# A relational graph network on one core: each node's edge to itself computed on chip, and ScalarE's copies of finished rows put ahead of the next tile's second exp

## The reference, cut to what matters

```python
for l in range(L):
    ht = jnp.einsum('nd,rdo->nro', h, W_rel[l])
    msg = ht[src, etype]
    h_rel = segment_sum(msg, dst) + h @ W_loop[l] + b_rel[l]
    z  = (h @ W_gat[l]).reshape(n, H, DH)
    el = sum(z * attn_l[l], -1);  er = sum(z * attn_r[l], -1)
    e  = leaky_relu(el[src] + er[dst], 0.2)
    ex = exp(e - segment_max(e, dst)[dst])
    h_gat = segment_sum(ex / denom * z[src], dst) + b_gat[l]
    hc = concat([h_rel, h_gat]) @ W_fuse + b_fuse
    if l == 0: hc = hc * sigmoid(concat([hc, mean(edge_weight)]) @ W_gate + b_gate)
    h = relu(hc)
x = layernorm(x + h)
```

## Time and profile before

| | us |
|---|---|
| time, median of 3 runs | 3487.19 (3486.21 to 3488.84) |
| profiled execution, span from first to last instruction | 3490.2 |
| POOL busy | 2489.3 (71%) |
| DVE busy | 2380.3 (68%) |
| PE busy | 689.4 (20%) |
| ACT busy | 424.8 (12%) |

### The profile page before, as it was taken

One profiled execution on the slowest core, in us unless ns is written; L12 is line 12 of the kernel. 1 busy time (PEld: TensorE's weight loads), 2 busy tenths in 40 slices (PEclk: granted clock), 3 DMA queues, 4 the chain that ended last, 5 costly groups with the idle time before them and its releaser, 6 DMA issues.

```text
span 3490.2 us, 18122 instructions
## 1 busy us (share of the span) xinstructions
PE 689.4 (20%) x1897; PEld 372.5 (11%) x1897; DVE 2380.3 (68%) x3226; ACT 424.8 (12%) x769; POOL 2489.3 (71%) x2642
## 2 busy tenths in 40 slices
PE   8942111222122230011121111221000000000000
PEld 5421000111011110000000000110000000000000
DVE  8536666677676764665777756674776788877786
ACT  3530110111111120101111111111000000000000
POOL 1457777777777756777777777775777777777776
PEclk9965555555655555555555555555555555555555
DMA  7774444455545544444454544454433333333332
GB/s 271 315 249 129 134 147 152 152 151 152 152 152 159 168 145 118 130 151 152 151 152 151 153 152 152 152 173 140 107 106 107 107 106 107 106 106 107 106 103 74
DMA packets 143244, 505.96 MB, mean 145 GB/s; under 512 B 44277, under 2 KB 51002, under 8 KB 133618
## 3 DMA queue, kind: packets, MB, share of 16 engines
q0 software_dynamic: 130032, 444.45, 43.4%
q1 hardware_dynamic: 13186, 61.24, 4.5%
HBM read 341.05 MB, written 164.51 MB: 145 GB/s over the span
## 4 chain that ended last, share of the span: by engine, by line
POOL 45%; issue 29%; DVE 10%; DMA 6%; PE 4%; POOLq 3%; DVEq 1%; ACT 1%; SPq 1%; ACTq 0%
POOL meta_nat L594 20%; POOL late L594 14%; POOL scratch L594 10%; DVE acc L1381 3%; PE ps_table L886 1%; DMA late<-table,stage_mid 1%; DMA table<-rows 1%; DMA scratch<-table,stage_tail 1%; DVE late L1377 1%; DVE scratch L1377 1%; DVE meta_nat L1377 1%; POOLq L369 1%; POOL table L671 1%; DMA meta_nat<-table,stage_head 1%; PE ps_cnt L919 1%
## 5 line engine op out<-in xcount | busy, mean ns | idle before, releaser
L594 POOL DMA_INDIRECT meta_nat<-table,stage_head x1200 | 1139.0, 949 | 395.7 <-issue 385.3
L594 POOL DMA_INDIRECT late<-table,stage_mid x720 | 681.9, 947 | 219.4 <-issue 217.9
L594 POOL DMA_INDIRECT scratch<-table,stage_tail x555 | 525.9, 948 | 175.5 <-issue 175.2
L1025 PE MATMUL ps_mix<-ident,hr 128*128 128x128 f32 x75 | 35.5, 473 | 1991.2 <-DVE hg L1401 1991.2
L788 ACT ACTIVATE ps_cnt<-logit 128x68 f32<-128x68 f32 x189 | 43.7, 231 | 2767.1 <-DVE logit L1363 2766.1
L1381 DVE TENSOR_REDUCE acc<-meta_nat 128x132 f32<-128x2112 f32 x75 | 290.6, 3875 | 8.1 <-DVE meta_nat L1377 0.5
L1371 DVE TENSOR_REDUCE acc<-meta_nat 128x128 f32<-128x2048 f32 x75 | 282.6, 3767 | 0.0
L1049 PE MATMUL ps_table<-wrel,hT 128*128 128x512 f32 x400 | 266.4, 828 | 0.0
L1353 DVE TENSOR_TENSOR raw<-late,er_cur 128x64 f32<-128x64 f32 x45 | 12.0, 267 | 324.5 <-DMA late<-table,stage_mid 324.5
L1025 PEld LDWEIGHTS ps_mix<-ident,hr 128*128 128x128 f32 x75 | 13.6, 182 | 2039.8 <-DVE hg L1401 2039.8
L1381 DVE TENSOR_REDUCE acc<-scratch 128x132 f32<-128x1188 f32 (+1 forms) x69 | 208.7, 3024 | 7.1
(11 more groups left out here) (237 smaller groups left out, 1701.4 us busy)
## 6 DMA issues: line engine op xcount, KB each, us to landing
table<-rows SPq DMA_DIRECT2D x25, 2080.0 KB, 7.7
meta_nat<-table,stage_head POOLq DMA_INDIRECT x1200, 2.8
late<-table,stage_mid POOLq DMA_INDIRECT x720
scratch<-table,stage_tail POOLq DMA_INDIRECT x555, 2.8
meta<-meta_ranked SPq DMA_DIRECT2D x1, 2438.0 KB, 15.1
wrel<-in_L_gnn_W_rel POOLq DMA_DIRECT2D x2, 1024.0 KB, 13.5
meta_nat<-in_x SPq DMA_DIRECT2D x1, 832.0 KB, 18.4
table<-rows,stage_id POOLq DMA_INDIRECT x50, 7.8
```

Source lines behind the costliest of these rows:

```text
L594: pool.indirect_dma_start(out=slots[b][:, k, :], out_offset=None, in_=table[l % 2], in_offset=bass.IndirectOffsetOnAxis(ap=index, axis=0)) ...
L1025: pe.transpose(mix[0], hr[:], ident[:])
```

## The change

Self edges are no longer gathered, except those of tile 0.

- While lists are prepared, DVE finds each node's last code, tests whether it is the node's own and whether its rank is at least 128, lowers the degree by one, puts the null row in its place and keeps the type in a new column `M_SELF`.
- The loop over all ranked tiles ahead of the layers is gone. In its place stands `first_layer_own`, which makes for one tile er, its own row of z and all 16 table products again from x, in ranked order. It runs for tiles 0 and 1 ahead of layer 0, and inside layer 0 at the end of each tile t for tile t+1.
- Of the 16 table products in PSUM, ACT keeps the one of the node's self type: 16 copies with a per-partition scale of 0 or 1 (`own_messages`). PE adds them and `h @ W_loop` in PSUM, 17 products (`own`), and ACT copies the sum to `meta` (`own_sum`). In layers 0 and 1 the same is done for the next layer, behind `next_rows`.
- The node's own z row is copied into slot 0 of H, which was unused, and the H group now has 17 slots in its logits and weighted sums.
- `next_rows` moves in ACT's order ahead of the exp of the second group. `s_rows` is incremented before the own copies.
- `z_product` of `next_table` is 136 columns wide rather than 264. The output buffer `yo` lies on `wrel`.

```diff
 (ACT)
-            act.wait_ge(s_meta, 16)
-            transposed_x(1)
-            for t in range(T):
-                if t < T - 1:
-                    transposed_x(t % 2)
-                act.wait_ge(s_er_ps, t + 1)
-                s.activation(meta[:, t, M_ER:META], ps_er[t % 2], ACT.Copy).then_inc(s_er, 1)
+            def own_er_and_z(t):
+                s.activation(meta[:, bass.ds(t, 1), M_ER:M_LOOP], ps_z[:, EL:ER]..., ACT.Copy)
+                s.activation(self_z[:, bass.ds(t, 1), :], ps_z[:, 0:EL]..., ACT.Copy)
+                s.activation(type_cur[:]..., self_type[:, bass.ds(t, 1), :], ACT.Copy)
+                s.activation(shut_cur[:], no_self[:, bass.ds(t, 1)], ACT.Copy).then_inc(s_type_cur, 1)
+                act.wait_ge(s_type_cur, n_own)
+                return s.activation(self_z[:, bass.ds(t, 1), DH:EL:EX], ps_z[:, DH:EL:EX]..., ACT.Identity,
+                                    bias=shut_cur[:])
+            def own_messages():
+                for r in range(R):
+                    m = s.activation(self_rows[:, r], ps_table[:, r * D:(r + 1) * D], ACT.Copy,
+                                     scale=type_cur[:, r:r + 1])
+                m.then_inc(s_masked, 1)
+            def own_sum(t, ready):
+                act.wait_ge(s_own_ps, n_own)
+                act.reg_add(n_own, n_own, 1)
+                s.activation(meta[:, bass.ds(t, 1), M_LOOP:META], self_sum..., ACT.Copy).then_inc(ready, 1)
+            def first_layer_own(t):
+                s.activation(x_cur[:]..., meta[:, bass.ds(t, 1), M_X:M_ELL], ACT.Copy).then_inc(s_x_cur, 1)
+                act.wait_ge(s_rank_xT, n_first)
+                s.activation(hT[1][:], xT_ranked, ACT.Copy).then_inc(s_hT[1], 1)
+                act.wait_ge(s_first_ps, n_first)
+                act.reg_add(n_first, n_first, 1)
+                own_er_and_z(t).then_inc(s_er, 1)
+                own_messages()
+                own_sum(t, s_own0)
...
                     s.activation(rows[0][:, :, D:ROW], bc(ps_z[:, 0:D + H], R), ACT.Copy)
-                    for j in range(2):
-                        evacuate_half(0, j)
-                    s.activation(meta[:, bass.ds(t, 1), M_ER:META], ps_z[:, D + H:ZW]..., ACT.Copy).then_inc(s_rows, 1)
+                    evacuate_half(0, 0)
+                    evacuate_half(0, 1).then_inc(s_rows, 1)
                     act.reg_add(n_tab, n_tab, 1)
+                    own_er_and_z(t)
+                    own_messages()
...
                     gate(l)
+                    next_rows(l, act.snap(n_last, min_val=0, max_val=T - 1))
                 with act.If(groups > 1):
                     group()
                     with act.If(groups > 2):
                         group()
-                if not first:
-                    next_rows(l, act.snap(n_last, min_val=0, max_val=T - 1))
-                    act.reg_add(n_last, n_last, 1)
...
+                elif l < L - 1:
+                    own_sum(act.snap(n_last, min_val=0, max_val=T - 1), s_own)
+                    act.reg_add(n_last, n_last, 1)
...
+            first_layer_own(0)
+            first_layer_own(1)
+            act.wait_ge(s_meta, 16)
...
+                if l == 0:
+                    with act.Fori(1, T - 1) as t:
+                        tile(l, t)
+                        first_layer_own(t + 1)
+                    tile(l, T - 1)
 (PE)
+            def own(l, k):
+                pe.wait_ge(s_masked, n_own)
+                pe.reg_add(n_own, n_own, 1)
+                pe.matmul(self_sum, hT[k][:], wz[:, l, ER:ZW], start=True, stop=False)
+                for r in range(R):
+                    mm = pe.matmul(self_sum, ident[:], self_rows[:, r], start=False, stop=r == R - 1)
+                mm.then_inc(s_own_ps, 1)
+            def first_layer_own():
+                pe.wait_ge(s_x_cur, n_x_cur)
+                pe.reg_add(n_x_cur, n_x_cur, 1)
+                pe.transpose(xT_ranked, x_cur[:], ident[:]).then_inc(s_rank_xT, 1)
+                pe.wait_ge(s_hT[1], n_hT[1])
+                pe.reg_add(n_hT[1], n_hT[1], 1)
+                pe.matmul(ps_z[:, 0:ER], hT[1][:], wz[:, 0, 0:ER], start=True, stop=True)
+                for c in range(4):
+                    mm = pe.matmul(ps_table[:, 512 * c:512 * c + 512], hT[1][:],
+                                   wrel[:, 0, c * RC * D:(c + 1) * RC * D], start=True, stop=True)
+                mm.then_inc(s_first_ps, 1)
+                own(0, 1)
...
                     pe.reg_add(n_tab, n_tab, 1)
+                    own(l + 1, 0)
...
-            for l in range(L):
+            with pe.Fori(2, T):
+                tile(0)
+                first_layer_own()
+            tile(0)
+            tile(0)
+            for l in range(1, L):
 (DVE, list preparation; lists and own are views of one chunk of tiles)
-                v.tensor_scalar(meta_nat[:, t0:t1, M_ELL:SCATTERED], ..., float(NULL), None, ALU.add).then_inc(s_ell_ok, 1)
+                step(v.tensor_tensor(codes, lists, is_last[:, t0:t1], ALU.mult))
+                step(v.tensor_reduce(code, codes, AX.X, ALU.add))
+                step(v.tensor_tensor(gap, code, self_at[:, t0:t1], ALU.subtract))
+                step(v.tensor_tensor(dropped[:, t0:t1], gap, gap, ALU.mult))
+                step(v.scalar_tensor_tensor(own, dropped[:, t0:t1], 0.25 * R * R, may_drop[:, t0:t1], ALU.is_lt, ALU.mult))
+                step(v.tensor_tensor(dropped[:, t0:t1], code, own, ALU.mult))
+                v.tensor_tensor(codes, is_last[:, t0:t1], bc_last(dropped[:, t0:t1], ELL), ALU.mult)
+                v.scalar_tensor_tensor(gap, gap, 0.5 * (R + 1), own, ALU.add, ALU.mult)
+                step(v.tensor_tensor(degree[:, t0:t1], degree[:, t0:t1], own, ALU.subtract))
+                v.tensor_scalar(meta_nat[:, t0:t1, M_SELF], gap, -1.0, None, ALU.add)
+                v.tensor_copy(meta_nat[:, t0:t1, M_CNT], degree[:, t0:t1])
+                v.scalar_tensor_tensor(lists, lists, float(NULL), codes, ALU.add, ALU.subtract).then_inc(s_ell_ok, 1)
 (DVE, layers; group works on slots 0 to K for H where it took 1 to K)
+                v.tensor_copy(slots["H"][:, 0:1, D:ROW], self_z[:, bass.ds(t, 1), :])
...
+                if l == 0:
+                    dve.wait_ge(s_own0, n_t)
```

More of the change, by code:

```diff
@@ L21 @@
 LEAST = -1.0e37
+SHUT = -1.0e34
 SLOPE = 0.2
@@ L46, in gnn_kernel @@
     META = M_LOOP + D
-    ZW = D + H + H + D
+    EL = D + H
+    ER = EL + H
+    ZW = ER + D
     HB = 25
@@ L121, in gnn_kernel @@
         rows = [sb(f"rows{i}", [P, R, ROW]) for i in range(2)]
+        self_z = rows[1][:].rearrange("p r f -> p (r f)")[:, 0:T * EL].rearrange("p (t f) -> p t f", f=EL)
+        assert T * EL <= R * ROW
+        self_rows = sb("self_rows", [P, R, D])
+        self_room = self_rows[:].rearrange("p r d -> p (r d)")
+        is_last = self_room[:, 0:T * ELL // 2].bitcast(BF16).rearrange("p (t j) -> p t j", t=T)
+        last_at, self_at, apart, may_drop, last_code, is_self, dropped = (
+            self_room[:, T * ELL // 2 + i * T:T * ELL // 2 + (i + 1) * T] for i in range(7))
+        assert T * ELL // 2 + 7 * T <= R * D
+        self_type = sb("self_type", [P, T, R])
+        no_self = sb("no_self", [P, T])
+        type_cur = sb("type_cur", [P, R])
+        shut_cur = sb("shut_cur", [P, 1])
+        x_cur = attn_tmp
         degree = sb("degree", [P, T])
@@ new lines, in own_messages @@
+            def own_messages():
[6 more added lines that the diff above has]
+                act.reg_add(n_own, n_own, 1)
+                s.activation(meta[:, bass.ds(t, 1), M_LOOP:META], self_sum.rearrange("p (o f) -> p o f", o=1), ACT.Copy
+                             ).then_inc(ready, 1)
@@ L859, in _ @@
                 tile(l, 0, first=True)
-                with act.Fori(1, T) as t:
-                    tile(l, t)
+                if l == 0:
[3 more added lines that the diff above has]
+                    tile(l, T - 1)
+                else:
+                    with act.Fori(1, T) as t:
+                        tile(l, t)
                 transposed(l)
@@ L864, in _ @@
                 gate(l)
-                next_rows(l, T - 1)
+                if l < L - 1:
+                    next_rows(l, T - 1)
+                    own_sum(T - 1, s_own)
         @block.tensor
@@ L998, in _ @@
                 natural_tile(t, t % 2, next_x=t < T - 1)
[L1001 to L1017 removed]
+            def first_layer_own():
[10 more added lines that the diff above has]
+                own(0, 1)
+            n_x_cur = counter(pe, "pe_x_cur", 1)
+            pe.wait_ge(s_rows, T + 1)
+            first_layer_own()
+            first_layer_own()
             pe.wait_ge(s_bload, 16 * (5 + 3 * L))
@@ L1173, in _ @@
             v.tensor_copy(meta_nat[:, :, M_START], starts[:])
-            step(v.tensor_tensor(ell_valid, bc(iota_slot[:], T), bc_last(degree[:], ELL), ALU.is_lt))
+            v.tensor_tensor(ell_valid, bc(iota_slot[:], T), bc_last(degree[:], ELL), ALU.is_lt)
```

(14 more changed lines are left out.)

87 lines of the change are left out of this document (52 added, 35 removed).

## The result

| | before | after |
|---|---|---|
| time, median us | 3486.7 (3485.4 to 3488.8, 4 runs) | 3531.7 (3526.9 to 3538.0, 4 runs) |
| ratio, 95% interval | | 1.0133 (1.0118 to 1.0147), slower |
| profiled execution, span | 3490.2 | 3525.3 |
| POOL, DVE, PE, ACT busy | 2489, 2380, 689, 425 | 2421, 2386, 1204, 804 |

The change costs 45.0 us by the runs and 35.1 by the two spans; the profiled execution after is the fastest of its four. The forecast was 3541, slower.

What follows compares the result with a forecast made beforehand. POOL's time to start DMAs was taken to bound the kernel before, with a longer ACT and PE chain in most layer 0 tiles after. -90 + 124 + 9 + 7 + 4 = +54 us, so 3541 us, range 3450 to 3630.

Steps and rivals of the forecast that it cites:

- Gathers, -90: All three layers: 24 fewer gathers in each, 72 x 1.252 = 90.1 us of POOL saved; layer 2 shows 28 to 31.
- Layer 0, +124 -30 = +94: Layer 0: an ACT and PE chain of 46 us (47.5 with three groups) exceeds POOL's time in 18 tiles, +124 us.
- the faster rival: Layer 0: PE at full clock everywhere and copies 0.17 us apart give a chain of 36 us; chance 0.24.
- The masked copies: ACT's 16 masked copies in layer 0: 0.25 us apart, the last 0.35, 4.1 us a set; bounds 2.7 and 5.8.
- Start, +9: Before layer 0: two own tiles put the first exp at 253 us, +9 us, bounds 2 and 14; list steps hidden.
- Ends, +7 and +4: Ends of layers 0 and 1: +7 us as the second exp waits for `next_rows`, and +4 us; bounds -5 and 15.
- The move of `next_rows`: ACT's order in the loops: the reorder alone costs nothing; a few us in each last tile if cover went.
- All slow: Layer 0: half clock throughout and copies at 0.36 us give a chain of 54 us, +221, 3708 us; chance 0.10.
- the gathers stay: Gather lists: each tile's largest list does not shrink, so the time is 3631 us; chance 0.02.
- Fits under POOL: Layer 0: a chain of 36 us gives about 3420 us, one of 40 gives 3451; faster below 42.8; chance 0.24.

Runs made afterwards that it cites:

- experiment 3: Changed kernel with one masked copy and two products everywhere, one of four wide table products in `first_layer_own`: 3422.9 us, ratio 0.9820 to the kernel before.
- experiment 2: `next_rows` put back behind the exps in the changed kernel: 3603.1 us; only `next_rows` moved ahead of the second exp in the kernel before: 3490.0 us.
- experiments 1, 3 and 4: Changed kernel with 15 of 16 masked copies and 15 of 17 products left out of `first_layer_own`: 3440.8 us; experiment 3; the edited kernel: 3431.1 us.
- the edited kernel: Changed kernel, all work kept, layer 0's table, copies and products handed over in parts, next tile's x copied and transposed ahead: 3431.1 us, ratio 0.9840.

## Why the prediction was right, step by step

Right: the sign, the place and the mechanism. The forecast was +54 us against +35 by the spans and +45 by the runs, 3541 against 3532. By the stretches above it said 18 us too much for layer 0, some 6 too much for the start and 3 for the end of layer 1, and took 7.5 us too much off layers 1 and 2. So part of the closeness is errors that cancel.

- *Gathers, -90.* 2403 are left. Where nothing is added, in layer 2, 27.4 us came of 30, just outside the 28 to 31 that was said; in layer 1, 25.0. What is missing in layer 1 is for the most part the loop of buffer H (experiment 3), which the prediction did not have: it took POOL's time for a tile as 1.252 a slot down to the last tile. In layer 1 the tiles of 26, 25 and 24 slots take 34.4 us each where that gives 33.9, 32.6 and 31.3.
- *Layer 0, +124 -30 = +94.* Measured +76.0. The round was put at 46 and 47.5 us and was 44.4 and 47.8. With these the same sum over the tiles is 107, and -30 + 107 = 77. The term was mis-sized by 1.6 us a round, over twelve two-group tiles.

| part of the round | said | measured |
|---|---|---|
| exp to hT | 7.6 | 7.5 |
| hT to the last table copy | 7.9 | 6.8 |
| small copies | 1.1 | 0.7 |
| masked copies | 4.1 | 4.2 |
| products, with handover | 6.6 | 6.9 |
| sum copy, x, transpose, hT | 1.5 | 1.3 |
| second z and table | 4.0 | 4.0 |
| small and masked copies, products | 11.8 | 11.8 |
| last product to the exp | 1.4 | 1.2 |
| sum | 46.0 | 44.4 |

Most of the 1.6 is the table behind hT. Its eight records took 4.97 us; in the tile of the earlier trace rows, from which the term was read, they had taken 6.07. PE had the higher clock more often, as the faster rival supposed (0.74 in layer 0 against 0.57), but to little use: in the three-group rounds the same table took 6.11 us, and the second one, put at the full clock, 5.1 where the two-group rounds had 3.60. A three-group round is 3.4 us longer than a two-group one, where 1.5 was said: ACT starts the copy of the sum 2.9 us after the products have ended in place of 0.2, since the third exp waits for DVE ahead of it.

- *The masked copies.* 16 in 4.24 us, 4.1 said. They start 0.25 us apart, as said; the first lasts 0.36 us and the last 0.49. By the Trainium skill, "ScalarE: Activation LUTs", section "What ACT_TABLE_LOAD costs", an estimate is 0.29 us from one to the next. The trace doesn't agree with that: 0.25 stands, and the sum with the page's figure would have been 24 us further off.
- *Start, +9.* Measured +2.5. Own tiles began at 211.2, not 214.5: ACT waited until then for the stores of the table and no longer. PE took the 16 products in 4.8 and 5.4 us. POOL went on at 254.48 against 251.61. The list steps took four passes of 0.9 us, but that they are covered held only just: the head indices were staged at 214.05 us, not 212 (207.63 before), and the trace now names that staging as what POOL's first gather waits for. The gather went from 214.45 to 214.94.
```profile
152.96 0.91 DVE L1359 TENSOR_TENSOR scratch<-meta_nat,self_rows 128x720 f32<-128x720 f32 x1
...
156.91 0.90 DVE L1370 SCALAR_TENSOR_TENSOR meta_nat<-meta_nat,scratch 128x720 f32<-128x720 f32 x1
...
213.88 0.17 DVE L1408 CAST stage_head<-meta 128x16 uint32<-128x16 f32 x1
...
214.94 0.95 POOL L620 DMA_INDIRECT meta_nat<-table,stage_head  x1 [8.01 <-DVE stage_head L1408]
```
- *Ends, +7 and +4.* Measured +8.0 and +1.0 between products. The end of layer 0 goes in the order that was said, against the earlier trace rows: exp, second exp behind the copies, hT, last store, first gather 47.1 us after the exp in place of 42.6, where 50 was said. So from the exp on it is 4.5 us; the other 3.5 of the 8.0 are there because before the last product stood 3.8 us behind its exp, after 0.3.
```profile
1355.17 0.23 ACT L845 ACTIVATE ps_cnt<-logit 128x68 f32<-128x68 f32 x1 [0.62 <-issue]
...
1374.24 0.36 ACT L845 ACTIVATE ps_cnt<-logit 128x68 f32<-128x68 f32 x1
...
1384.65 0.23 DVE L1554 TENSOR_SCALAR hT<-th 128x128 f32<-128x128 f32 x1
...
1393.37 0.98 POOL L697 DMA_INDIRECT table<-rows,stage_id  x1 [22.57 <-issue]
...
1402.26 0.98 POOL L620 DMA_INDIRECT meta_nat<-table,stage_head  x1 [7.91 <-issue]
```
- *The move of `next_rows`.* "Nothing in the loops" held for the kernel before (experiment 2). The prediction did not say what it is worth in the changed kernel, which is 71 us: the order that is free under POOL is the main thing once the chain of ACT and PE is the bound.
- *The rivals.* "All slow" and "the gathers stay" fell. "Fits under POOL" was right about its condition: with the chain short enough the kernel is faster, 3423 to 3441 us in experiments 1, 3 and 4, within its 3420 to 3451. The chain of the change itself, 44.4 us and more, was too long for that.

## What to carry to other kernels

Work that goes to idle engines is free only if they can do it side by side: add up the round of everything that takes turns from one tile to the next, and hold that, not the busy shares, against the bounding engine's time for its shortest tile. If the round is the longer, first hand over in smaller parts and move what doesn't depend on the tile ahead; here this was worth 101 us with all the work kept. And when the bounding engine is relieved, ask what lies just under it: one slot less gave 1.25 us a tile only down to the 34.4 us in which the one buffer H is filled, used and freed.

## What the runs showed that was not expected

- In a condition that was there for over an hour, on three chips, and gone an hour and a half after it was last seen, the kernel before took 3965 to 3980 us in place of 3487 (+14%), the changed one 4617 (+31%), the edited one 4354 to 4376 (+27%), while single instructions lasted the same (a gather 0.947 us, a masked set 4.22). ACT stood still for up to 57 us with its inputs ready; in eleven stretches of the changed kernel's layer 0 it went on 5.4 to 6.5 us after POOL's gathers stopped. Whether instructions or something else came late to it the traces don't tell. It is no property of one chip: one of the three had run the kernel before at 3486 us just earlier, another did so later. A comparison holds only beside a run of the kernel before at the same time, and even its ratio did not carry over: 1.013 became 1.165.
- PE's clock changes within a round and not only between stages. The same 16 products took 5.86 and 6.00 us in the two-group rounds, where PE had waited for ACT (granted clock 0.62 and 0.60), and 3.93 (clock 1.00) when they ran behind the table in the edited kernel.
